# Self attention in a decoder layer: all float32 products of a unit in one block on TensorE, with the weights turned three units behind

## What is computed

```python
q = rotary(einsum('bpd,hde->bphe', x, W_Q) + b_Q)      # k likewise
v = einsum('bpd,hde->bphe', x, W_V) + b_V
scores = where(causal, q @ k.T / sqrt(128), 0)
max_v = max(abs(scores), -1)
sgn = sign(scores)
attn_w = sgn * exp(sgn * scores - max_v)
attn = attn_w / (sum(abs(attn_w), -1) + 1e-6)
out = einsum('bqhd,hdm->bqm', attn @ v, W_O) + b_O
```

## Time and profile before

| | |
|---|---|
| median of 3 runs | 1419.06 us (1418.25 to 1420.79) |
| the profiled execution | 1421.1 us, of which the span from first to last instruction is 1418.7 |
| TensorE busy | 1372.0 us (97%) |
| VectorE busy | 1193.5 us (84%) |
| ScalarE busy | 815.5 us (57%) |
| GpSimd busy | 657.8 us (46%) |
| mean granted TensorE clock | 0.989 of full speed |
| moved by DMA | 79.94 MB, 56 GB/s |

### The profile page before, as it was taken

One profiled execution on the slowest core, in us unless ns is written; L12 is line 12 of the kernel. 1 busy time (PEld: TensorE's weight loads), 2 busy tenths in 40 slices (PEclk: granted clock), 3 DMA queues, 4 the chain that ended last, 5 costly groups with the idle time before them and its releaser, 6 DMA issues.

```text
span 1418.7 us, 25443 instructions
## 1 busy us (share of the span) xinstructions
PE 1372.0 (97%) x8610; PEld 1087.5 (77%) x8610; DVE 1193.5 (84%) x1982; ACT 815.5 (57%) x1826; POOL 657.8 (46%) x746
## 2 busy tenths in 40 slices
PE   8999999999999999999999999999999999988895
PEld 6888888888888888888888888887777777532332
DVE  6888888888888888888887888856778889899997
ACT  6454544445454544455555656745556555687996
POOL 6534435245334443443523533752245544576763
PEclk9999999999999999999999999999999999998999
DMA  7300201011010110020112203210000003313434
GB/s 282 120 16 31 68 8 45 30 46 45 30 45 15 45 60 15 16 69 29 52 46 76 74 27 113 91 60 31 16 6 12 14 15 114 92 37 75 97 86 104
DMA packets 73316, 79.94 MB, mean 56 GB/s; under 512 B 45942, under 2 KB 46454, under 8 KB 72828
## 3 DMA queue, kind: packets, MB, share of 16 engines
q1 hardware_dynamic: 73212, 78.73, 18.5%
HBM read 59.83 MB, written 8.40 MB: 48 GB/s over the span
## 4 chain that ended last, share of the span: by engine, by line
PE 78%; DVE 12%; issue 6%; POOL 2%; ACT 1%; DMA 1%; SPq 0%; DVEq 0%; POOLq 0%; ACTq 0%
PE psum L358 16%; PE psum L360 16%; PE psum L359 16%; PE psum L1108 4%; PE psum L423 4%; PE psum L402 4%; PE psum L1110 3%; PE psum L1109 3%; PE psum L411 3%; DVE hn L1939 3%; DVE fsmall L1945 2%; PE psum L1202 2%; PE psum L425 2%; PE psum L400 2%; PE psum L1214 1%
## 5 line engine op out<-in xcount | busy, mean ns | idle before, releaser
L864 POOL TENSOR_TENSOR qk<-rope_a,rope_b 128x512 f32<-128x512 f32 x128 | 177.1, 1383 | 495.9 <-DVE rope_b L589 495.9
L358 PE MATMUL psum<-x_hi,w_hi 128*128 128x512 f32 x512 | 210.4, 411 | 1.5 <-DVE x_lo L530 1.5
L360 PE MATMUL psum<-x_hi,w_lo 128*128 128x512 f32 x512 | 201.4, 393 | 0.0
L359 PE MATMUL psum<-x_lo,w_hi 128*128 128x512 f32 x512 | 200.5, 392 | 0.0
L589 DVE SCALAR_TENSOR_TENSOR rope_b<-psum,qk_bias,sin 64x512 f32<-64x512 f32 x256 | 192.0, 750 | 3.7
L713 ACT ACTIVATE e<-s 128x384 f32<-128x384 f32 x128 | 66.3, 518 | 208.2 <-DVE s L570 208.2
L358 PE MATMUL psum<-w_hi,x_hi 128*128 128x256 f32 x512 | 147.5, 288 | 1.2 <-DVE v L612 1.2
L360 PE MATMUL psum<-w_hi,x_lo 128*128 128x256 f32 x512 | 144.8, 283 | 0.0
L359 PE MATMUL psum<-w_lo,x_hi 128*128 128x256 f32 x512 | 144.7, 283 | 0.0
L727 ACT ACTIVATE e<-p 128x128 f32<-128x128 f32 x128 | 39.3, 307 | 176.1 <-DVE p L598 176.1
L632 DVE TENSOR_TENSOR acc<-psum,acc 128x512 f32<-128x512 f32 x128 | 88.6, 692 | 59.8 <-PE psum L360 44.0
(11 more groups left out here) (198 smaller groups left out, 3768.6 us busy)
## 6 DMA issues: line engine op xcount, KB each, us to landing
stage<-w_self_dram SPq DMA_DIRECT2D x64, 256.0 KB, 2.8
w_raw<-w_ffn_dram SPq DMA_DIRECT2D x32, 512.0 KB, 3.6
acc<-x_dram SPq DMA_DIRECT2D x4, 1024.0 KB, 6.0
w_signs<-w_sign SPq DMA_DIRECT2D x16, 256.0 KB, 2.1
xw_raw<-w_cross_dram SPq DMA_DIRECT2D x4, 1024.0 KB, 5.5
c_raw<-ctxT_dram SPq DMA_DIRECT2D x8, 512.0 KB, 3.5
w<-w_signs SPq DMA_DIRECT2D x2, 2048.0 KB, 12.0
out_dram<-yb SPq DMA_DIRECT2D x16, 256.0 KB, 2.1
```

The costliest lines, as they stand in the source:

```text
L358: pe.matmul(ps, ah, bh, start=n == 0, stop=False)
L359: pe.matmul(ps, ah, bl, start=False, stop=False)
L360: last = pe.matmul(ps, al, bh, start=False, stop=n == len(pairs) - 1)
L864: nc.gpsimd.tensor_tensor(qk[:, k % 2, which, :], rope_a[:, which, :], rope_b[:, which, :], ALU.add).then_inc(qk_ready, 1)
```

## The change

**p gets a second buffer**: p is a pair (p_even, p_odd), chosen by the unit's parity, in `turn`, `times_sign`, `totals` and `norm`. `times_sign` now waits for the turn of two units back instead of one.

**TensorE**: turning and mixing move from unit t-2 to unit t-3, and all float32 work of a slot stands at its start: turn 0, score 0, score 1, turn 1, mix 0, mix 1, and then Q, [odd: output 0], K, [odd: output 1], [even: output 0], V, [even: output 1]. The drain follows the same order. In slots 1 and 2 Q still comes first.

**VectorE**: times_sign 0 and 1 move ahead of rope Q, and z_low moves from before v_out to behind times_sign.

**ScalarE**: both take_turned come first in the slot, then the V and O weight pieces; z_high moves behind the exponentials, and the Q and K pieces behind it. The rounding of the context in slot 64 stays where it is in the text, which is now behind both take_turned.

```diff
-        p = sb("p", [P, 2, LW])
+        p_even = sb("p_even", [P, 2, LW])
+        p = (p_even, sb("p_odd", [P, 2, LW]))
...
# tensor
+            def turn_and_mix(t, k):
+                turn(t - 3, k - 3, 1)
+                mix(t - 3, (k - 3) % 8, 0)
+                mix(t - 3, (k - 3) % 8, 1)
...
+                if live(t, 3):
+                    turn(t - 3, k - 3, 0)
                 if live(t, 1):
                     score(t - 1, k - 1, 0)
                     score(t - 1, k - 1, 1)
-                if live(t, 2):
-                    turn(t - 2, 0)
+                if live(t, 3):
+                    turn_and_mix(t, k)
                 if live(t, 0) and not second:
                     project(t, k, 0)
-                if live(t, 2):
-                    turn(t - 2, 1)
                 if odd and o_live(t, k):
                     output(t, k, 0)
                 if live(t, 0):
                     project(t, k, 1)
                 if odd and o_live(t, k):
                     output(t, k, 1)
-                if live(t, 2):
-                    mix(t - 2, (k - 2) % 8, 0)
-                    mix(t - 2, (k - 2) % 8, 1)
...
# vector
-                wait(dve, turned, (u - 1) * 2 + b + 1)
-                nc.vector.tensor_tensor(p[:, b, :], e[:, b, :], sgn[:, b, :], ALU.mult).then_inc(p_ready, 1)
+                wait(dve, turned, (u - 2) * 2 + b + 1)
+                nc.vector.tensor_tensor(p[k % 2][:, b, :], e[:, b, :], sgn[:, b, :], ALU.mult).then_inc(p_ready, 1)
...
                     mask_and_max(t - 1, 1)
-                if live(t, 3):
-                    z_low(t - 3, (k - 3) % 8)
-                if live(t, 1):
                     v_out(t - 1, (k - 1) % 8, v_bias[:, bass.ds(group(t, k, i, 1) * 256, 256)])
...
-                elif live(t, 0):
+                if live(t, 1):
+                    times_sign(t - 1, k - 1, 0)
+                    times_sign(t - 1, k - 1, 1)
+                if live(t, 3):
+                    z_low(t - 3, (k - 3) % 8)
+                if live(t, 0) and not opening:
                     rope(t, k, 0, bass.ds(group(t, k, i) * 2 + k % 2, 1))
                 if odd and o_live(t, k):
                     add_output(t, k, 0)
-                if live(t, 1):
-                    times_sign(t - 1, 0)
-                    times_sign(t - 1, 1)
...
# scalar
+                if live(t, 3):
+                    take_turned(t - 3, 0)
+                    take_turned(t - 3, 1)
                 if i is not None:
                     next_pieces(t, k, i)
-                if live(t, 3):
-                    z_high(t - 3, (k - 3) % 8)
                 if t == UNITS:
                     passage["round_context"]()
                 if live(t, 1):
                     abs_and_sign(t - 1, 0)
-                if live(t, 2):
-                    take_turned(t - 2, 0)
-                if live(t, 1):
                     exps(t - 1, 0)
                     abs_and_sign(t - 1, 1)
                     exps(t - 1, 1)
-                if live(t, 2):
-                    take_turned(t - 2, 1)
+                if live(t, 3):
+                    z_high(t - 3, (k - 3) % 8)
+                if i is not None:
+                    next_projections(t, k, i)
```

More of the change, by code:

```diff
@@ L403, in score, with turn @@
                           start=True, stop=True).then_inc(scores, 1)
-            def turn(u, b):
+            def turn(u, k, b):
                 if isinstance(u, int) and u == 0 and b == 0:
@@ L410, in turn @@
                 for n in range(3):
-                    last = pe.transpose(psT[:, n * P:(n + 1) * P], p[:, b, n * P:(n + 1) * P], ident[:])
+                    last = pe.transpose(psT[:, n * P:(n + 1) * P], p[k % 2][:, b, n * P:(n + 1) * P], ident[:])
                 last.then_inc(turned, 1)
@@ L483, in emit @@
                 second = isinstance(t, int) and t in (1, 2)
+                if isinstance(t, int) and t >= UNITS:
+                    drain(t, k)
+                    return
                 if second:
                     project(t, k, 0)
+                if isinstance(t, int) and i == SCALED_IN and k == 0:
+                    pe.wait_ge(w_meaned, 1)
+                if live(t, 3):
+                    turn(t - 3, k - 3, 0)
                 if live(t, 1):
@@ L488, in emit @@
                     score(t - 1, k - 1, 1)
[L489 to L493, removed]
-                if live(t, 2):
-                    turn(t - 2, 0)
+                if live(t, 3):
+                    turn_and_mix(t, k)
+                if isinstance(t, int) and i == SCALED_IN and k == 7:
+                    total_weights()
                 if live(t, 0) and not second:
                     project(t, k, 0)
-                if live(t, 2):
-                    turn(t - 2, 1)
                 if odd and o_live(t, k):
@@ L721, in exps, with totals @@
                                      ).then_inc(e_ready, 1)
-            def totals(u, b):
+            def totals(u, k, b):
                 act.wait_ge(p_ready, u * 2 + b + 1)
                 wait(act, total_guard, (u - 1) * 2 + b + 1)
-                nc.scalar.activation(e[:, b, 0:P], p[:, b, 0:P], ACT.Abs, accum_out=total[:, b, 0:1])
-                nc.scalar.activation(e[:, b, P:LW], p[:, b, P:LW], ACT.Abs, accum_out=total[:, b, 1:2]
+                part = p[k % 2][:, b, :]
+                nc.scalar.activation(e[:, b, 0:P], part[:, 0:P], ACT.Abs, accum_out=total[:, b, 0:1])
+                nc.scalar.activation(e[:, b, P:LW], part[:, P:LW], ACT.Abs, accum_out=total[:, b, 1:2]
                                      ).then_inc(total_ready, 1)
@@ L794, in next_pieces, with next_projections @@
                     for n in (O0, O1):
+                        round_piece(i + 1, n)
+            def next_projections(t, k, i):
+                if k in (7, 0):
+                    act.wait_ge(qk_proj, (t - 1) * 2 + 2)
+                    for n in (Q0, K0) if k == 7 else (Q1, K1):
                         round_piece(i + 1, n)
@@ L870, in norm @@
                     n = cols.stop - cols.start
-                    last = nc.gpsimd.tensor_tensor(p[:, b, cols], p[:, b, cols],
+                    last = nc.gpsimd.tensor_tensor(p[k % 2][:, b, cols], p[k % 2][:, b, cols],
                                                    inv[:, b, rows:rows + 1].broadcast_to([P, n]), ALU.mult)
```

25 lines of the change are left out of this document (8 added, 17 removed).

## The result

The changed kernel takes **1451.82 us** (median of 4 runs, 1450.16 to 1452.52) beside 1419.03 for the kernel before (1418.25 to 1420.79): a ratio of 1.0219, with an interval of 1.0206 to 1.0233. It is slower, inside the range and 8 us above the forecast. The profiled execution took 1452.52 us with a span of 1450.2, which is 31.5 more than the span before; the sum had +24.6. The kernel before was run again beside the experiments: its median was 1420.6 us beside e1 to e4 and 1420.72 beside e5 to e7, where one of its 29 runs took 3475.5 us, in the slow state, and is left out of the ratios.

The account below looks back on a forecast made before the run. It took TensorE's issue rate in self attention as the bound; 9.8 - 3 + 3 + 7.8 + 5 + 2 = +24.6 us on the profiled 1421.1 gave 1445.7, or 1444 for the median. Range: 1426 to 1456.

Parts of the forecast that it names:

- mix 1 waits for copy 1: TensorE's new block: only one mix covers ScalarE's second copy, so 0.15 us idle in each unit, +9.8 us.
- switches: TensorE: three float32 runs a slot become one, saving 0.05 us in each of 62 slots, -3 us.
- odd slots, output 1: TensorE's output 1 waits 0.1 us for VectorE's addition in each of 30 odd slots, +3 us (0 to 9).
- roundings, 14 slots: At k=0 and k=4 two weight roundings behind copy 1 delay the chain, +0.56 us in 14 slots, +7.8 us.
- jumps, less the old wait: VectorE's idle time at loop jumps delays output 1; 6.7 less 1.6 of old turn waits, +5 us (1 to 9).
- opening and drain: Opening net -0.8; in the drain cross attention's first projection waits for the late context rounding; sum about +2 us.
- The rival that only this wait counts: The ScalarE and VectorE chain has 0.3 us more slack, so other terms shrink: 1426 to 1432 us, chance 0.20.
- The reading that capped it: TensorE's slot over its bare products of 14.35 us: odd 0, even 0.10 above, so at most 6 us saved.
- the rival that went faster: Switches between kinds of product cost more than seen and copy 1 ends within mix b=0: 1410 us, chance 0.09.
- The chain through ScalarE and VectorE: From copy 1 through exponentials, sign products and rope to the odd slot's addition, ending at 10.22 us, output 1 at 10.37.
- The sign products: On VectorE, ahead of the rope: mean falls from about 0.9 towards 0.55, busy time by some 70 us, no gain.
- the rival that they still meet GpSimd: VectorE's sign products take 1.05 us each, adding 0.55 to the chain in 44 slots: 1468 us, chance 0.06.

Follow-up runs that it names:

- e1: Changed kernel with turn 1 placed between the two products of score 1: 1434.41 us, ratio 1.0093 to the kernel before.
- e4: Changed kernel with VectorE's slots written out in full instead of two loops, so no jump: 1442.44 us, ratio 1.0152.
- e5: Changed kernel with e1, e3 and e4 together, weight and context roundings moved ahead of or between copies, scale_weights one slot earlier: 1417.88 us, ratio 0.9978.
- e7: Kernel before the change with only VectorE's slots written out in full: 1419.78 us, ratio 0.999.
- e6: e5 with both mixes moved behind Q, making two float32 runs a slot instead of one: 1420.15 us, ratio 0.9994.
- e3: Changed kernel with z's low part behind the first addition in odd slots, on VectorE: 1445.23 us, ratio 1.0174.
- e2: Changed kernel with ScalarE's V and O weight roundings ahead of both copies, as before the change: 1443.35 us, ratio 1.0158.

## Why the prediction came out 8 us low

Over slots 5 to 63, 59 of the 64, the length grew by 28.3 us; up to slot 5 it fell by 1.7; from the last score to cross attention's first transposes (947.57 before, 977.65 after) it grew by 3.5. This makes 30.1, and 1.4 more came from there to the end, the feed-forward part included, where no experiment was made. Kernels with the same code there differ as much from one profile to the next (471.15 us in e6, 472.55 after; 471.13 before), so the 1.4 needs no cause in the change. Of the 8 us by which the forecast was low, 6.9 are in the span (31.5 against 24.6); the other 1.3 come from taking the profiled execution to be 2.0 above the median, where it was 0.7 above (1452.52 and 1451.82). By the terms of the sum:

| term | forecast | measured | from |
|---|---|---|---|
| mix 1 waits for copy 1 | +9.8 | +10.6 (59 x 0.18) | mixes above, e1 |
| switches | -3 | -1.7 (29 x 0.06) | even slots, e1, e6 |
| odd slots, output 1 | +3 | +2.6 | first product, e3 |
| roundings, 14 slots | +7.8 | +7.7 | k=4 and k=0 slots, e2 |
| jumps, less the old wait | +5 | +7.9 | slots, e4, e7 |
| opening and drain | +2 | +1.8 | -1.7 and +3.5 |
| w_mean, slots 39 and 40 | 0 | +0.6 | slots, e5 |

The first five rows and the last give 27.7 of the 28.3 us. The sixth row agrees in part by luck: the opening gained 1.7 where 0.8 was forecast, and the drain lost 3.5 where the parts of the sum had 2.6.

1. **The block's wait: right, slightly small.** I had the copy at 0.46; in the block it lasts 0.48, and the restart is in two parts, 0.08 late and 0.10 slow. It is 0.18 and not 0.15. The rival that only this wait counts (1426 to 1432) fell: the chain has no slack. e5 shows that the rest can be removed too, and e1 that this wait is the largest part, 17.4 us with what it passes on to the odd and the k=0 and k=4 slots, 1.7 of them in slot 53, where the clock stayed at the lower level for 3.4 us instead of 6.8.
2. **Switches: right in kind.** The saving was measured with the wait taken away: 0.10 in even slots, -0.02 in odd ones (e1 against before). In the changed kernel itself it reads as 0.06 in even slots, and I had counted 0.05 in both. The reading that capped it, slot length less bare products, was the step that held; the rival that went faster fell with it.
3. **The chain through ScalarE and VectorE: right within 0.02 us at its stations there.** It was built from rows of the old order alone, end to end, with each engine's queue put in the new order. The exception is its last step, back to TensorE: output 1 was to begin at 10.37 of an odd slot and begins at 10.29 (467.48), not late at all, and the 0.1 stands in its slow first product instead; that term's size is right partly by luck. The chain gave the 0.53 of the k=0 and k=4 slots (0.56 forecast), the odd slots' wait, and c_lo's. The old timetable had no such row.
4. **The jumps: the step that failed.** The waits were sized right: slots 13, 21 and 29 are 1.37, 1.26 and 1.21 above a plain odd slot (1.2 forecast), slot 53 waits for 3.4 (3.1). I took a wait's cost to be its length. In slot 53 the granted clock halved behind it, and this is 2.6 of the 2.9 us that the term lacked. Slot 53 of the kernel before had no sign of it: it idled for 1.61 us there and was 1.9 longer. But the opening of the same trace had one, at the longest of the three waits of the earlier trace rows, and I had read only its length. TensorE's row, then two windows of the kernel before, columns as above:

```profile
35.21 0.88 PE L411 MATMUL psum<-ident,p 128*128 128x128 f32 x3 [2.75 <-ACT pT L734]
...
35.00:36.00 1.00, 0.79 (x4) 0.82 (x5) 1.00 (x3) 1.00 (x4) 1.00 (x2) 0.57 0.00 0
36.00:38.00 2.00, 2.00 (x6) 1.54 (x6) 0.09 (x1) 1.76 (x5) 2.00 (x3) 0.50 0.09 13
```

The clock is at the 1.2 GHz level from 35.2 to 38.6. In slot 53 the fall came with idle times of 1.96 us (e2, a microsecond after TensorE had started again), 2.99 (e1), 3.11 (e3) and 3.25 (after), and in no slot 13, 21 or 29, where they were 0.5 to 1.5. In e1 to e3 it lasted some 3.4 us, in the kernel after 6.8. The length of a wait doesn't decide alone: ahead of slot 3's score TensorE idled for 2.80 to 2.87 us in e1 to e6, and the clock fell in e2, e5 and e6 and not in e1, e3 and e4; at the wait for c_lo it fell in e1 (2.25 us), e2 and e4 (2.50) and not in e3 and the kernel after (2.50 too).

5. **The wait for w_mean was missed.** It stood behind the two scores before, ahead of turn 0; now turn 0 comes first in the slot, and the wait with it. I had listed who waits for the copies and the additions, but not what else the moved step waits for. It cost 0.6 us, nearly all removed in e5 (slot 39: 14.57).
6. **The sign products** fell from a mean of 0.98 to 0.64, median 0.56, and the rival that they still meet GpSimd (1468) is refuted. The busy time fell by 36 us and not by 70; my own two figures, 0.9 and 0.55 for 128 of them, would have given 45. The Trainium skill's rule in "SBUF — State Buffer" (practical consequences) fits: beside a rope addition of GpSimd two took 2.11, away from it each takes 0.56. The long ones that are left are in the opening and the drain, each beside a GpSimd operation: 1.22 beside a rope addition in slot 1, 3.88 in slot 2, begun beside a weight split and run on beside a rope addition, 1.30 in slot 3 beside the splitting of x, up to 1.12 beside the splitting of cross attention's weights. In the k=0 and k=4 slots the first of the two takes 0.76 beside a weight split, and behind it VectorE idles until the second half of e is there. So in the loops' slots TensorE sees nothing of it, as the prediction said.

On the jump the Trainium skill has two sentences that lead to different times. "Advanced Engine Details and Errata" (Control Flow Timing) gives about 108 ns for a compare-and-branch; VectorE is idle for 2.93 and 5.11 us instead, and 9.4 to 9.8 us of this kernel hung on it (e4). "Runtime: NRT & Kernel Launch" (Instruction fetch mechanics) says that a taken branch whose target lies outside the fetched window must load it first. It gives no price for that. It fits that writing out the loop removes the idle time (e4, e7); no run here shows the fetch itself.

**Left open:** why products are slower in a slot with one more run of float32 work; what decides, beside the length of a wait, whether the clock falls; and what the block alone gains over a whole execution. Slots 5 to 63 take 851.95 us in the kernel before, 849.95 in e7 and 847.67 in e5: the jump gives 2.0 there, and the block with e5's other edits 2.3 more. Up to cross attention's transposes e5 loses 1.8 of that again in the opening and the drain, and begins them at 944.93 against 945.41 in e7. The medians of the two, 11 runs each, are 1.9 apart, and their ranges overlap. So most of e5's 2.8 us against the kernel before can be the jump's. The wait of mix 1 wasn't taken away by itself (e1 moves the whole chain forward as well), nor were the roundings of the context and the wait for w_mean tried apart from e5.

## What to carry to other kernels

Putting all work of one kind together is worth at most what the slots have over their bare products, here 0.10 us in every other slot, and it takes away the cover of every hand-over between the pieces: list each (turn, copy, mix) with its wake, its length and its restart, and put other work of that kind between them before the block is built. Moving a step also moves what it waits for and what its queue holds up on the other engines; the whole chain can be worked out from the old trace to a few hundredths of a us. A loop's jump that costs nothing in one order can cost 10 us in another, because the wait then reaches TensorE, and a TensorE that has idled for some 2 to 3 us may come back at half its clock. The trace of before can show that: read the granted clock behind its longest waits, and not only their length.

## What the runs showed of the hardware that I had not expected

- Behind a wait of 3.25 us TensorE's granted clock was at the 1.2 GHz level, which cost 2.6 us on top. Waits of 0.5 to 1.6 us in slots 5 to 63 had no such effect, one of 1.96 (e2) brought 3.4 us at the lower level, and waits of 2.2 to 2.9 had it in some kernels and not in others.
- VectorE stands idle for 2.9 to 3.2 us at a jump of the first loop and for 4.3 to 5.6 at that of the second, in all five kernels that have the loops (before, after, e1, e2, e3), and not at all in those without (e4 to e7).
- A wait of TensorE that ends before the modelled end of the instruction ahead of it carries no label, and the first product behind a wait is longer by 0.07 to 0.10 us: 0.18 us in each unit left no row in the list of waits.
- One float32 run more in a slot cost 0.08 us in even and 0.04 in odd slots (e6), yet the kernel before, with three, has shorter odd slots than e6 with two.
